# One kernel of attention and quantised FFN on one core: where the FFN bias enters, how Wo is multiplied, how the probabilities are turned, and how gate and gain are formed

## The reference

```
h   = einsum('bct,bcd->bdt', x, weights[condition])          # a 32x32 mixing matrix per batch
qkv = h @ Wqkv + bqkv                                        # three times 128 columns
a   = softmax(q k^T / sqrt(128))                             # 32 x 32 within a batch
x   = x + (a v) @ Wo + bo                                    # Wo is 128 x 512
y   = sum over t < length of x / length                      # one number per row of x
g   = sigmoid(conv1d(y, 5 taps))
z   = x * g
out = x + bf16(mx(z) @ mx(weight)^T + bias)                  # mx: fp8 e4m3 with a power-of-two scale per 32 elements
```

## Time and profile before

| | |
|---|---|
| runs of the kernel, us | 132.89, 134.19, 638.56 (median 134.19) |
| the profiled execution, us | 134.14 |
| its span, us | 132.5 |
| mean granted TensorE clock (1 is 2.4 GHz) | 0.974 |
| busy: TensorE, VectorE, ScalarE, GpSimd, us | 115.1, 109.3, 56.7, 40.3 |

### The profile page before, as it was taken

One profiled execution on the slowest core, in us unless ns is written; L12 is line 12 of the kernel. 1 busy time (PEld: TensorE's weight loads), 2 busy tenths in 40 slices (PEclk: granted clock), 3 DMA queues, 4 the chain that ended last, 5 costly groups with the idle time before them and its releaser, 6 DMA issues.

```text
span 132.5 us, 2651 instructions
## 1 busy us (share of the span) xinstructions
PE 115.1 (87%) x732; PEld 80.6 (61%) x732; DVE 109.3 (83%) x266; ACT 56.7 (43%) x139; POOL 40.3 (30%) x65
## 2 busy tenths in 40 slices
PE   5996799798999899999999999999988968439870
PEld 2342689685995787589577858985854733123420
DVE  5529997929999989998997899799989979999640
ACT  4130516334553363366337525633642370372440
POOL 5641154441536305342615312230220220220500
PEclk9999999999999999999999999999999999955999
DMA  4989687149776963989997999949690396252563
GB/s 69 370 275 206 242 179 202 19 70 239 142 138 113 261 177 59 186 266 187 235 185 206 190 247 181 239 88 187 62 289 11 79 215 105 26 80 52 76 129 117
DMA packets 21799, 21.20 MB, mean 160 GB/s; under 512 B 12901, under 2 KB 12904, under 8 KB 21784
## 3 DMA queue, kind: packets, MB, share of 16 engines
q0 software_dynamic: 5344, 8.77, 38.9%
q1 hardware_dynamic: 15458, 10.66, 29.0%
q10 hardware_dynamic: 982, 1.59, 4.8%
HBM read 6.85 MB, written 7.86 MB: 111 GB/s over the span
## 4 chain that ended last, share of the span: by engine, by line
PE 44%; DVE 14%; issue 5%; ACT 3%; DVEq 0%; ACTq 0%
PE ps_qk L442 10%; PE ps_v L455 8%; PE ps_ffn L539 7%; PE ps_wo L497 6%; PE ps_mix L429 5%; DVE h_sum L949 3%; PE ps_ffn L537 2%; ACT h_mag L653 2%; DVE h_round L956 2%; DVE h_floor L937 2%; PE ps_att L479 2%; DVE masked L855 1%; DVE x L846 1%; DVE h_min L961 1%; PE ps_att L469 1%
## 5 line engine op out<-in xcount | busy, mean ns | idle before, releaser
L442 PE MATMUL ps_qk<-xc,wqkv_f 128*128 128x256 f32 x128 | 30.2, 380 | 1.6 <-ACT xc L640 1.6
L442 PEld LDWEIGHTS ps_qk<-xc,wqkv_f 128*128 128x128 f32 x128 | 24.0, 190 | 8.3 <-issue 5.2
L391 POOL DMA_DIRECT2D out_dram<-ffn_out x14 | 12.1, 866 | 40.1 <-ACT ffn_out L705 39.9
L284 POOL DMA_DIRECT2D mix_w<-in_L_cond_weights_dram x29 | 15.0, 518 | 20.7 <-issue 20.7
L497 PE MATMUL ps_wo<-wo_f,o_t 128*128 128x512 f32 x30 | 15.8, 607 | 1.9 <-ACT o_t L660 1.4
L455 PE MATMUL ps_v<-wqkv_f,xc 128*128 128x128 f32 x128 | 17.2, 280 | 0.0
L429 PE MATMUL ps_mix<-mix_w,x_sb 128*128 128x128 f32 x128 | 15.9, 276 | 1.4 <-DMA mix_w<-in_L_cond_weights_dram 1.4
L384 POOL DMA_DIRECT2D x_sb<-bo_row x8 | 9.8, 1222 | 22.7 <-PE ps_mix L429 22.7
L705 ACT ACTIVATE ffn_out<-ps_ffn 128x512 bf16<-128x512 f32 x14 | 8.4, 597 | 19.4 <-PE ps_ffn L539 19.4
L455 PEld LDWEIGHTS ps_v<-wqkv_f,xc 128*128 128x128 f32 x128 | 15.9, 192 | 0.8
L429 PEld LDWEIGHTS ps_mix<-mix_w,x_sb 128*128 128x128 f32 x128 | 15.1, 192 | 2.0 <-issue 1.9
(11 more groups left out here) (80 smaller groups left out, 138.5 us busy)
## 6 DMA issues: line engine op xcount, KB each, us to landing
x_sb<-bo_row POOLq DMA_DIRECT2D x8, 512.0 KB, 6.1
x_sb<-in_x_dram SPq DMA_DIRECT2D x7, 512.0 KB
out_dram<-x SPq DMA_DIRECT2D x14, 256.0 KB, 4.2
out_dram<-ffn_out POOLq DMA_DIRECT2D x14, 256.0 KB, 3.7
ffn_w_f<-in_L_ffn_weight_dram ACTq DMA_DIRECT2D x2, 512.0 KB, 4.3
wqkv_f<-in_L_attn_Wqkv_dram POOLq DMA_DIRECT2D x1, 768.0 KB, 7.1
x_sb<-in_x_dram SPq DMA_DIRECT2D x2, 256.0 KB, 4.6
mix_w<-in_L_cond_weights_dram SPq DMA_DIRECT2D x32, 4.0 KB, 2.9
```

The costliest lines, as they stand in the source:

```text
L284: queue.dma_start(mix_w[C * j:C * (j + 1), u, t, C * j:C * (j + 1)], cond_w[bass.ds(k, 1)].rearrange("k c d -> (k c) d")) \
L391: nc.gpsimd.dma_start(out_v[SUB * u + t], ffn_out[:, u % 2, t, :], accum_op=ALU.add).then_inc(added[u % 2][t], 16)
L442: mm = nc.tensor.matmul(ps_qk[:, which, :], wqkv_f[:, c, which * D:(which + 1) * D], xc[:, u % 2, c, :], start=(c == 0), stop=(c == TC - 1))
```

## The change

Five things change.

- The FFN has two banks, `ps_ffn[t]`, one for each tile of a unit. TensorE writes both once at the start with a filler matmul (`open_ffn_banks`). Ahead of each use ScalarE copies the bias, broadcast over the partitions in f32, into the bank (`seed_bias`), and the four matmuls of `ffn` add to it; the bias matmul and all that made `bias_rows` go. GpSimd issues the broadcast DMA of the bias ahead of `add_bo(1)`. `ps_tr` goes; transposes of the last two units go to `ps_v` and to the `ps_mix` banks.
- Wo and the attention output are each split in a high and a low part of type float32r (`split_wo` on ScalarE and `low_wo` on VectorE once; `copy_o` on ScalarE and `low_o` on VectorE per unit). `project_out` makes three matmuls: high by high, high by low, low by high.
- The probabilities are turned by one transpose over 128 partitions, then spread over the four diagonal blocks by one product with the mask `own_batch`, which also writes the zeros.
- gate_den holds eg + 1 and (eg + 1) / 2^20, and one reciprocal gives gate and gain.
- ScalarE's order: copy_ffn(s-3, 1) stands behind magnitude(s+1) of the next step, the two seeds behind copy_mix.

```diff
-        ps_tr = pb("ps_tr", [P, TC, TOK], BF16)
-        ps_ffn = pb("ps_ffn", [P, N], F32)
+        ps_ffn = [pb(f"ps_ffn{t}", [P, N], F32) for t in range(SUB)]
...
-            def spread_bias():
...
-                if u == 3:
-                    spread_bias()
...
-            nc.gpsimd.memset(prob_t[:], 0.0).then_inc(prob_t_zeroed, 1)
-            nc.gpsimd.memset(ones[:], 1.0).then_inc(ones_done, 1)
-            nc.gpsimd.dma_start(bias_col[:], ffn_b.rearrange("(p k) -> p k", p=P)) \
-                .then_inc(bias_loaded, 16)
...
             gather_mix_w(nc.gpsimd, 3, 1)
+            nc.gpsimd.dma_start(bias_row[:], ffn_b.partition_broadcast(P)).then_inc(bias_loaded, 16)
             add_bo(1)
...
+            def open_ffn_banks():
+                for t in range(SUB):
+                    nc.tensor.matmul(ps_ffn[t][:], warm[:, 0:P], warm[:], start=True, stop=True) \
+                        .then_inc(ffn_banks_opened, 1)
...
-                    pe.wait_ge(o_done, u)
+                    pe.wait_ge(o_lo_done, u)
...
-                nc.tensor.matmul(wo_bank(u, t), o_t[:, tok], wo_f[:], start=True, stop=True) \
+                nc.tensor.matmul(wo_bank(u, t), o_hi[:, tok], wo_hi[:], start=True, stop=False)
+                nc.tensor.matmul(wo_bank(u, t), o_hi[:, tok], wo_lo[:], start=False, stop=False)
+                if t == 0:
+                    pe.wait_ge(o_lo_done, u + 1)
+                nc.tensor.matmul(wo_bank(u, t), o_lo[:, tok], wo_hi[:], start=False, stop=True) \
                     .then_inc(wo_done, 1)
...
-                nc.tensor.matmul(bank, ones[:], bias_rows[:], start=True, stop=False)
+                pe.wait_ge(bias_seeded, SUB * u + t + 1)
                 for c in range(TC):
...
-            act.wait_ge(warm_zeroed, 1)
-            nc.scalar.activation(bias_rows[:], warm[:], ACT.Copy).then_inc(bias_rows_zeroed, 1)
...
-                    act.wait_ge(gain_done, v - WBLOCKS + 1)
+                    act.wait_ge(gate_done, v - WBLOCKS + 1)
...
-                nc.scalar.activation(o_t[:], ps_o, ACT.Identity, bias=bqkv_sb[:, 2:3]) \
-                    .then_inc(o_done, 1)
+                nc.scalar.activation(o_hi[:], ps_o, ACT.Identity, bias=bqkv_sb[:, 2:3]) \
+                    .then_inc(o_hi_done, 1)
+            def split_wo():
+                act.wait_ge(wo_loaded, 16)
+                nc.scalar.activation(wo_hi[:], wo_f[:], ACT.Copy).then_inc(wo_hi_done, 1)
...
+            def seed_bias(u, t):
+                if u == 0:
+                    act.wait_ge(bias_loaded, 16)
+                    act.wait_ge(ffn_banks_opened, t + 1)
+                else:
+                    act.wait_ge(ffn_out_done, SUB * (u - 1) + t + 1)
+                nc.scalar.activation(ps_ffn[t][:], bias_row[:], ACT.Copy).then_inc(bias_seeded, 1)
...
                 magnitude(s + 1, 1)
+                if s >= 3:
+                    copy_ffn(s - 3, 1)
                 copy_o(s)
...
+                if s >= 2:
+                    seed_bias(s - 2, 0)
+                    seed_bias(s - 2, 1)
                 copy_qk(s + 1)
...
-                if s >= 2:
-                    copy_ffn(s - 2, 1)
...
             copy_o(UNITS - 1)
+            seed_bias(UNITS - 3, 0)
+            copy_ffn(UNITS - 4, 1)
+            seed_bias(UNITS - 3, 1)
             copy_ffn(UNITS - 3, 0)
+            seed_bias(UNITS - 2, 0)
             exp_gate(UNITS - 1)
             copy_ffn(UNITS - 3, 1)
+            seed_bias(UNITS - 2, 1)
...
-                nc.vector.transpose(prob_t[p, :, p], prob_n[p]).then_inc(prob_t_done, 1)
+            def softmax_turn(u):
+                dve.wait_ge(prob_n_done, u + 1)
+                nc.vector.transpose(prob_q[:].rearrange("p t q -> p (t q)"),
+                                    prob_n[:].rearrange("p t k -> p (t k)")).then_inc(prob_q_done, 1)
+            def softmax_spread(u):
...
+                nc.vector.tensor_tensor(prob_t[:].rearrange("p t (j q) -> p t j q", j=JB),
+                                        prob_q[:].unsqueeze(2).to_broadcast([P, SUB, JB, C]),
+                                        own_batch[:].unsqueeze(1).unsqueeze(3)
+                                        .to_broadcast([P, SUB, JB, C]), ALU.mult) \
+                    .then_inc(prob_t_done, 1)
+            def low_wo():
+                dve.wait_ge(wo_hi_done, 1)
+                nc.vector.tensor_tensor(wo_lo[:], wo_f[:], wo_hi[:], ALU.subtract) \
+                    .then_inc(wo_lo_done, 1)
+            def low_o(u):
+                dve.wait_ge(o_hi_done, u + 1)
+                nc.vector.scalar_tensor_tensor(out=o_lo[:], in0=ps_o, scalar=bqkv_sb[:, 2:3],
+                                               in1=o_hi[:], op0=ALU.add, op1=ALU.subtract) \
+                    .then_inc(o_lo_done, 1)
...
+                nc.vector.scalar_tensor_tensor(out=gate_den[:],
+                                               in0=eg[:, u % 2].unsqueeze(1).to_broadcast([P, 2, SUB]),
+                                               scalar=1.0,
+                                               in1=gate_k[:].unsqueeze(2).to_broadcast([P, 2, SUB]),
+                                               op0=ALU.add, op1=ALU.mult).then_inc(gate_den_done, 1)
...
+                nc.vector.reciprocal(gates[:], gate_den[:]).then_inc(gate_done, 1)
...
                 round_sum(s + 1, 0)
+                low_o(s)
                 round_sum(s + 1, 1)
```

More of the change, by code:

```diff
@@ L104, in adaln_attn_ffn_kernel @@
         bo_row = sb("bo_row", [P, 1, T], F32)
[L105 to L109, removed]
+        bias_row = sb("bias_row", [P, N], F32)
         warm = sb("warm", [P, T], BF16)
@@ L139, in adaln_attn_ffn_kernel @@
         prob_n = sb("prob_n", [P, SUB, C], F32)
+        prob_q = sb("prob_q", [P, SUB, C], F32)
         prob_t = sb("prob_t", [P, SUB, P], F32)
-        o_t = sb("o_t", [P, TOK], F32)
+        own_batch = sb("own_batch", [P, JB], F32)
+        wo_hi = sb("wo_hi", [P, T], F32R)
+        wo_lo = sb("wo_lo", [P, T], F32R)
+        o_hi = sb("o_hi", [P, TOK], F32R)
+        o_lo = sb("o_lo", [P, TOK], F32R)
         masked = sb("masked", [P, SUB, T], F32)
         ysum = sb("ysum", [P, SUB], F32)
-        gate_den = sb("gate_den", [P, SUB], F32)
-        gate = sb("gate", [P, SUB], F32)
+        gate_den = sb("gate_den", [P, 2, SUB], F32)
+        gates = sb("gates", [P, 2, SUB], F32)
+        gate = gates[:, 0, :]
+        gain = gates[:, 1, :]
+        gate_k = sb("gate_k", [P, 2], F32)
         amax = sb("amax", [P, 2, SUB, NB], F32)
@@ L207, in adaln_attn_ffn_kernel @@
         bq_done = sem("bq_done")
[L208 to L211, removed]
+        ffn_banks_opened = sem("ffn_banks_opened")
+        bias_seeded = sem("bias_seeded")
         mix_done = sem("mix_done")
@@ L522, in ffn @@
                             pe.wait_ge(xq_turned[v][n], 16)
-                    for k in range(len(PART_ROWS)):
-                        pe.wait_ge(bias_done[k], 16)
-                    pe.wait_ge(ones_done, 1)
                 if u < UNITS - WBLOCKS:
@@ L1014, in _ @@
             block_max(1, 1)
-            bias_parts()
             block_limits(1)
@@ L1018, in _ @@
             score_max(0)
+            low_wo()
             round_sum(1, 0)
@@ L1021, in _ @@
             softmax_divide(0)
-            for j in range(JB):
-                softmax_turn(0, j)
+            softmax_turn(0)
+            softmax_spread(0)
             round_sum(1, 1)
             round_back(1)
+            low_o(0)
             residual_sum(0, 0)
@@ L1038, in _ @@
                 softmax_divide(s)
-                for j in range(JB):
-                    softmax_turn(s, j)
+                softmax_turn(s)
+                softmax_spread(s)
                 block_limits(s + 1)
@@ L1058, in _ @@
             softmax_divide(UNITS - 1)
-            for j in range(JB):
-                softmax_turn(UNITS - 1, j)
+            softmax_turn(UNITS - 1)
+            softmax_spread(UNITS - 1)
             block_limits(UNITS)
             floor_step(UNITS)
+            low_o(UNITS - 1)
             round_sum(UNITS, 0)
```

113 lines of the change are left out of this document (46 added, 67 removed).

## The result

| | before, same chip | changed |
|---|---|---|
| median, us | 133.83 (4 runs, one of them 638.56) | 129.32 (4 runs, 128.89 to 129.8) |
| profiled execution, us | 134.14 | 129.8 |
| its span, us | 132.5 | 128.0 |

The ratio is 0.968, 95% interval [0.964, 0.972]: faster, by 3.7 to 4.8 us of 133.8. Forecast were 130.7 us and a range of 129.2 to 133.2; the median lies in the range, 0.1 from its lower end.

What follows compares the result with a forecast made beforehand. TensorE was taken to bound four steps at 12.1 us, VectorE 0.5 behind. Steps 3 to 6 -2.1, step 2 -0.1, prologue -0.2, tail -0.5, -0.17 and -0.4 sum to -3.5: 134.2 becomes 130.7 us, range 129.2 to 133.2.

Steps and rivals of the forecast that it cites:

- Steps 3 to 6: Main-loop steps, gate_den to gate_den: from 12.10 to 11.58 us each, -2.1 us for the four.
- the wait in front of h_floor: VectorE's idle 0.56 us per step, waiting for ScalarE's h_mag: goes, since copy_ffn now stands behind h_mag.
- Then a tile takes 0.65 instead of 0.86: Output projection on TensorE: three float32r matmuls of 0.215 us replace one f32 matmul; -0.43 for two tiles.
- The turn and the spread: VectorE, per step: four transposes (1.07 us) become one of 0.27 with its wait plus a 0.43 spread; -0.37.
- all six steps: Sign in the main loop: gate_den to gate_den takes 11.4 to 11.75 us in every step.
- the chain mixed of VectorE and TensorE: Sign in the profile: the chain of waits runs through both engines, where before it was TensorE alone.
- Step 1, "nothing": First main-loop step: no gain, since both halves of v precede the projection and o_hi comes 0.2 us late.
- Prologue and tail: Before and after the main loop: prologue -0.2 us with the table load's move covered; tail -0.5, -0.17 and -0.4.
- rival 2: TensorE's clock stays low in the tail, eight last FFN matmuls at 0.43 instead of 0.215: +1.7, 132.4 us; chance 0.09.
- (1): o_hi comes later still and VectorE stalls 0.45 us at low_o in every step: 132.4 us; chance 0.18.
- (3): The transpose over 128 partitions goes by partitions: +0.7 us in each of 7 VectorE steps, 135.6 us; chance 0.06.
- (4): float32r on TensorE takes more than one pass, deciding from 0.36 us per matmul: 135.4 or 154 us; chance 0.07.

Runs made afterwards that it cites:

- the control: The changed kernel itself measured again with no edit, compared with the kernel before: median 130.28 us, ratio 0.969 [0.962, 0.975].

## Why the prediction was right, and where it was not

**What held.** Direction and size: -3.5 us forecast, -4.3 by the ratio. The median of 129.32 is just below the forecast's own range, 129.4 to 131.8; by the ratio, from the 134.2 it reckoned with, it would be 129.9. Steps 3 to 6 were put at 11.58 and took 11.54 (-2.1 forecast, -2.2 measured), step 2 -0.1 and -0.28. The bias matmul is worth 0.43 a step, one transpose over 128 partitions goes by columns (246 ns), the gates save 0.2, the wait in front of h_floor goes, low_o stalls 0.15 where 0.1 was counted, the seeds cost ScalarE 0.6 each and nobody else (it still idles 0.76 in front of the q copy), and the table load moves and costs nothing that the times show. The Trainium skill's rule that the table is loaded right before the first ACTIVATE (page ScalarE: Activation LUTs, section Step-by-step: what each stage is for, on the table-load gate) agrees with the trace: 8.35 here and 1.97 with the added activation, both directly ahead of the first one.

**What failed: "Then a tile takes 0.65 instead of 0.86".** It takes 0.70, 0.23 a matmul, so TensorE saved 0.32 a step. The three records are there, each 0.015 to 0.02 longer than a bf16 one. (For the f32 product the Trainium skill, page FP8 and Floating Point Precision, section TensorE Precision Notes, counts four passes; the trace agrees, 0.86 being four times 0.215.) So TensorE's loop, put at about 11.45, is 11.54. The turn and the spread were mis-sized the other way (0.62 for 0.70), and VectorE's own work is 11.38 for 11.45. The forecast of 11.58 came near 11.54 because 0.13 for stall and jitter had been added to both; that this covered the 0.09 missing on TensorE is luck.

**What failed more: the worth of the Wo part.** The sum gave Wo 0.43 on TensorE and 0.42 on VectorE and let both count towards one step of 11.58. The runs show that part as a loss: 1.3 us gained by taking it out of the change, 2.0 us lost by putting it on the kernel before, and nothing either way once both loops are open. On TensorE the saved 0.32 is met by 0.16 more wait ahead of the scores (0.12 to 0.28), as the text foresaw; on VectorE low_o counts in every step and lies in the loop with o_hi. "Against" the rival of the slow float32r the forecast asked only whether three passes beat two records, not whether the saving pays for low_o. The overall forecast survived because bias and turn bring 5.3 us between them. Of the signs named, "all six steps" missed step 1, and "the chain mixed of VectorE and TensorE" missed as well: through step 5 it is TensorE's alone.

**Step 1, "nothing".** +0.38 in the second profile. h_mag of unit 0 stands behind copy_v(1), and VectorE, faster by turn and gates, now comes to it 0.75 early; putting it ahead takes 0.4 off the step (11.89 to 11.47). The other 0.89 us of the first profile is one late DMA transpose, which other kernels here show in other steps.

**Prologue and tail.** -0.2 forecast ahead of step 1, -0.81 seen; 0.77 of it is the landing of the mixing weights, which varies by 1.2 us between profiles, so the profiles cannot tell. The tail was put at -1.07 and came to -1.48 in the first profile, and to nothing in the control's (22.18 against 22.19), most of the difference by the clock (rival 2). The -1.48 is made up thus: from gate_den to h_floor -1.04 (turn, gates and the wait of 0.46, 1.02 forecast), low_o and its neighbours +0.27 (0.42), the clip -0.2 (0.17), the FFN to the final sum -0.51 (0.4). Not in the forecast were the 0.89 us between the last final_sum and the end, in which the last store lands; no edit touches it, and the kernel before with float32r Wo alone has 3.3 there too instead of 4.2, so it is not the change's.

**The rivals.** (1) no: the stall is 0.15, not 0.45; with the bias matmul back it is 0.32. (2) not in the first profile, but yes in the control's. In the first, TensorE's clock is low in the tail as before (0.50 from 113 to 119 us, where the eight FFN matmuls of unit 6 take 3.44 us) and full again before the last eight:

```profile
122.00:124.00 2.00, 2.00 (x13) 0.90 (x12) 0.21 (x1) 1.19 (x2) 0.00 (x0) 1.00 0.94 147
```

```profile
122.09 1.89 PE L526 MATMUL ps_ffn<-wq_t,xq_t 128*128 128x512 bf16 x8
```

In the control the clock stays at 1.00 through the FFN of unit 6 and is 0.50 from 121 to 124 us, after a wait of 2.37, and the last eight matmuls take 3.21:

```profile
121.23 0.61 PE L511 MATMUL ps_mix<-ident,xq 128*128 128x128 bf16 x4 [2.37 <-DVE xq L989]
121.63 3.21 PE L526 MATMUL ps_ffn<-wq_t,xq_t 128*128 128x512 bf16 x8
```

That is 1.3 of the 1.5 us by which its tail is longer. It is the one profile of the fourteen in which the last FFN ran at the low clock; how often it happens in the executions without a profile is not known.

(3) no, by the 246 ns. (4) no by its size (0.23, under the 0.36 from which it decides), though for Wo by itself its sign was right, by another mechanism. (Its sum for 0.43 a matmul comes to 135.5, not 135.4.)

## What to carry to other kernels

When two engines are nearly full, price an edit that moves work from one to the other by both loops, and undo each part of a bundle once: a part can be a loss inside a change that is a gain. An idle stretch is room only if what ends it does not itself depend on that engine's last step, so follow the waited-for instruction back before filling it. And profile the same kernel twice before believing a tail: here two profiles differ by 1.5 us there. Put an independent instruction between two dependent ones: here low_o cost 0.21 us there instead of 0.40.

## What the runs showed of the hardware

- A float32r matmul of 128 columns by 512 takes 0.23 us from start to start, a bf16 one 0.215, an f32 one 0.86 in two records of 0.43.
- Behind the pair of h_sum, VectorE starts h_round, which depends on it, 0.19 us later than o_lo, which doesn't (1.52 against 1.33), and o_lo fits in between.
- After a long wait for the mixing weights TensorE's clock was low (1.2 GHz, 0.50) in two prologues. The first row is from 16 to 20 us of the kernel with Wo in f32 again, whose TensorE had waited 2.05 us; the second, at the full clock, is of the one with gate and gain apart, which had waited 1.91:

```profile
16.00:20.00 4.00, 3.62 (x9) 2.94 (x10) 3.84 (x13) 1.40 (x5) 2.34 (x3) 0.50 0.82 197
```

```profile
16.00:20.00 4.00, 3.66 (x18) 3.28 (x19) 3.83 (x13) 1.87 (x6) 2.37 (x3) 1.00 0.88 215
```

The 16 matmuls of the q/k projection took 6.00 us instead of 3.69, some 2.3 us more. The second low one is the changed kernel with the early table load (2.14 us of wait, 6.16). The mixing weights came no later there (first mix at 12.98 and 13.33) than in profiles at the full clock (up to 13.59); TensorE had finished its fillers earlier. The kernel before with float32r alone had waited 1.94 at the full clock. In the tail, the control's clock was low after a wait of 2.37. These are four profiles and not an experiment: that the wait is the cause is not shown, and whether more filler matmuls would prevent it was not tried.
